# Start-up loads issued from two queues, a high part written in one step, and paced gathers for the second expert in a one-core mixture-of-experts kernel

## The reference, cut to what matters

```python
xprev = concat([shift_state[:, None, :], x[:, :-1]], axis=1)
xk = x + (xprev - x) * time_maa_k
xr = x + (xprev - x) * time_maa_r
e_idx = token_ids * 5099 % 16                 # expert of each of the 8192 tokens
pos = rank of the token within its expert     # kept if pos < 512
expert_in = xk scattered to (16 experts, 512 slots, 512)
h = square(relu(expert_in @ w_key[e]))        # 512 -> 1024
expert_out = h @ w_value[e]                   # 1024 -> 512
r = sigmoid(xr @ w_recept)                    # 8192 x 512 by 512 x 512
out = x + r * expert_out[slot]                # 0 for a token that was dropped
```

## Time and profile before

| | before |
|---|---|
| median of three runs | 886.61 us (886.07 to 887.07) |
| the profiled execution | 886.43 us, of which the span from the first to the last instruction is 884.7 us |
| PE busy | 878.2 us of the span, granted clock 1.0 throughout (the 2.4 GHz level) |
| DVE, ACT, POOL busy | 653.4, 499.4, 502.1 us |
| DMA | 186.40 MB, mean 211 GB/s |

### The profile page before, as it was taken

How to read it: one execution, slowest core, us unless ns; L and a number is a source line. 1 busy time by engine, 2 the same in 40 slices (tenths; PEclk the granted TensorE clock), 3 DMA queues, 4 the chain that set the end, 5 groups by cost and what they waited for, 6 DMA issues and landing times.

```text
span 884.7 us, 10918 instructions
## 1 busy us (share of the span) xinstructions
PE 878.2 (99%) x3963; PEld 726.6 (82%) x3963; DVE 653.4 (74%) x894; ACT 499.4 (56%) x773; POOL 502.1 (57%) x471
## 2 busy tenths in 40 slices
PE   8999999999999999999999999999999999999998
PEld 7888888888888888888888888888888888888887
DVE  6987746859687777777787878787877777777742
ACT  7766656565556464646464737373737282828270
POOL 2000034465676777676767676767676767674142
PEclk9999999999999999999999999999999999999999
DMA  6675568675757575757575757575757565756341
GB/s 240 223 264 194 194 213 281 228 256 164 252 181 252 189 251 186 253 183 251 184 249 180 250 184 244 185 249 185 244 185 243 194 241 190 243 188 223 119 143 47
DMA packets 72533, 186.40 MB, mean 211 GB/s; under 512 B 10400, under 2 KB 10656, under 8 KB 72480
## 3 DMA queue, kind: packets, MB, share of 16 engines
q1 hardware_dynamic: 44672, 101.79, 34.1%
q0 software_dynamic: 27664, 83.91, 28.1%
q10 hardware_dynamic: 144, 0.00, 0.0%
HBM read 152.11 MB, written 33.55 MB: 210 GB/s over the span
## 4 chain that ended last, share of the span: by engine, by line
PE 98%; DMA 0%; issue 0%; DVE 0%; ACT 0%; SPq 0%; POOLq 0%; POOL 0%
PE acc L914 29%; PE acc L916 29%; PE acc L915 29%; PE rt_bank L916 3%; PE rt_bank L914 3%; PE rt_bank L915 3%; PE acc L926 1%; DMA xT<-xs_t 0%; PE rt_bank L994 0%; POOLq L99 0%; POOL out L446 0%; DVE mix L769 0%; ACT mix L502 0%; ACT xr_hi L510 0%; DVE gate L837 0%
## 5 line engine op out<-in xcount | busy, mean ns | idle before, releaser
L431 POOL DMA_INDIRECT pair_even<-pairs,row_pair x128 | 144.6, 1130 | 174.9 <-DVE row_pair L743 105.3
L543 ACT ACTIVATE hid<-acc 128x512 f32<-128x512 f32 x112 | 67.1, 600 | 208.3 <-PE acc L916 208.2
L431 POOL DMA_INDIRECT pair_odd<-pairs,row_pair x128 | 144.9, 1132 | 58.3 <-issue 32.9
L915 PE MATMUL acc<-wv_lo,h_hi 128*128 128x512 f32 (+1 forms) x456 | 176.6, 387 | 0.0
L916 PE MATMUL acc<-wv_hi,h_lo 128*128 128x512 f32 (+1 forms) x456 | 176.6, 387 | 0.0
L914 PE MATMUL acc<-wv_hi,h_hi 128*128 128x512 f32 (+1 forms) x456 | 176.6, 387 | 0.0
L914 PE MATMUL acc<-xk_hi,wk_hi 128*128 128x512 f32 x448 | 174.6, 390 | 0.0
L916 PE MATMUL acc<-xk_hi,wk_lo 128*128 128x512 f32 x448 | 174.5, 390 | 0.0
L915 PE MATMUL acc<-xk_lo,wk_hi 128*128 128x512 f32 x448 | 174.3, 389 | 0.0
L780 DVE TENSOR_TENSOR wv_lo<-raw,wv_hi 128x1024 fp32r<-128x1024 f32 x64 | 78.4, 1226 | 59.5 <-ACT wv_hi L531 59.5
L808 DVE TENSOR_TENSOR h_lo<-hid,h_hi 128x512 fp32r<-128x512 f32 x128 | 88.4, 691 | 35.2 <-ACT h_hi L552 35.2
(11 more groups left out here) (148 smaller groups left out, 1507.3 us busy)
## 6 DMA issues: line engine op xcount, KB each, us to landing
raw<-w_key SPq DMA_DIRECT2D x64, 512.0 KB, 5.5
raw<-w_value SPq DMA_DIRECT2D x64, 512.0 KB, 3.8
xT<-xs_t SPq DMA_DIRECT2D x13, 1026.0 KB, 7.6
gates<-gate SPq DMA_DIRECT2D x8, 1024.0 KB, 5.5
gates<-wr_raw SPq DMA_DIRECT2D x8, 1024.0 KB, 5.3
xT<-xs_t SPq DMA_DIRECT2D x11, 256.5 KB, 5.4
pair_even<-pairs,row_pair POOLq DMA_INDIRECT x128, 3.1
pair_odd<-pairs,row_pair POOLq DMA_INDIRECT x128, 2.9
```

Source lines behind the costliest of these rows:

```text
L431: pool.indirect_dma_start(pair[e % 2][:, i, :], None, pairs, bass.IndirectOffsetOnAxis(row_pair[:, a:a + 1], 0)).then_inc(s_pair[e % 2], 16)
L543: act.activation(hid[:, n % H_SLOTS, :], up_bank(*divmod(n, KF))[:, :], ACT.Relu).then_inc(s_relu, 1)
L915: pe.matmul(bank, hi, m_lo, start=False, stop=False)
```

## The change

It has two parts. At the start, W0 and W1 are issued by ACT, around `maar`, in place of SP, so SP's list is L, R, X1, X2, W2, X3, W3 and so on. DVE writes the high part of the left half directly (the same sum once more, with a rounded output) ahead of writing it to `mix`; POOL, which rounded it, now rounds the right half of W0's chunk, which DVE did. DVE takes `mix_xr(0)` ahead of `split_w_recept(0)`, and PE takes the right half's high by high product ahead of the left half's with `wr_lo`. In the middle, the 16 gathers of the second expert wait, eight per five chunks, for PE's chunks of groups 14 and 15 and its first three blocks of expert 0; PE counts the chunks on a new semaphore `s_chunk`, where `s_R` doesn't.

```diff
             sp.dma_start(xT[:, 0, 0, 0:1 + HALF], xs_t[0:P, 0:1 + HALF]).then_inc(s_x_left, 16)
-            load_w_recept(0)
-            load_group(0, 0)
-            for k in range(1, KD):
+            for k in range(KD):
                 load_group(0, k)
-                load_w_recept(k)
+                if k > 1:
+                    load_w_recept(k)
...
-            pool.wait_ge(s_mix_left, 1)
-            pool.tensor_copy(xr_hi[:, 0, 0, 0:HALF], mix[:, 0, 0:HALF]).then_inc(s_hi_left, 1)
+            pool.wait_ge(s_wrec[0], 16)
+            pool.tensor_copy(wr_hi[:, 0, D // 2:D], wr_raw[:, 0, D // 2:D]).then_inc(s_wrhi_first, 1)
...
+                    elif e == 1:
+                        at = 1 + 5 * i // 8
+                        if at < KD - 1:
+                            pool.wait_ge(s_chunk, at + 1)
+                        elif at == KD - 1:
+                            pool.wait_ge(s_R, ST * (G - 1))
+                        elif at < 2 * KD - 1:
+                            pool.wait_ge(s_chunk, at)
+                        elif at == 2 * KD - 1:
+                            pool.wait_ge(s_R, ST * G)
+                        else:
+                            pool.wait_ge(s_U, at - 2 * KD + 1)
...
+            act.dma_start(wr_raw[:, 0, :], w_recept_t[0:P, :]).then_inc(s_wrec[0], 16)
             act.dma_start(maar[:, :], maa_r[:, :]).then_inc(s_maar, 16)
+            act.dma_start(wr_raw[:, 1, :], w_recept_t[P:2 * P, :]).then_inc(s_wrec[1], 16)
...
                 dve.wait_ge(s_maar, 16)
+                dve.scalar_tensor_tensor(xr_hi[:, 0, 0, 0:HALF], slot, factor, here,
+                                         ALU.mult, ALU.add).then_inc(s_hi_left, 1)
                 dve.scalar_tensor_tensor(slot, slot, factor, here, ALU.mult, ALU.add).then_inc(s_mix_left, 1)
...
             mix_left()
-            dve.wait_ge(s_wrec[0], 16)
-            dve.tensor_copy(wr_hi[:, 0, D // 2:D], wr_raw[:, 0, D // 2:D]).then_inc(s_wrhi_first, 1)
             split_left()
+            mix_xr(0)
             dve.wait_ge(s_wrhi_first, 1)
             split_w_recept(0)
-            mix_xr(0)
...
+                pe.wait_ge(s_hi_right, 1)
+                first_pass(0, right, xr_hi, wr_hi, True)
                 pe.wait_ge(s_wrlo, 1)
                 first_pass(0, left, xr_hi, wr_lo)
-                pe.wait_ge(s_hi_right, 1)
-                first_pass(0, right, xr_hi, wr_hi, True)
                 first_pass(0, right, xr_hi, wr_lo)
...
+                if g + 2 >= G and k < KD - 1:
+                    mm.then_inc(s_chunk, 1)
```

More of the change, by code:

```diff
@@ L280, in moe_token_shift @@
         s_step = sem("s_step")
+        s_chunk = sem("s_chunk")
         s_sq = sem("s_sq")
@@ L760, in split_left @@
                 dve.wait_ge(s_hi_left, 1)
+                dve.wait_ge(s_mix_left, 1)
                 dve.tensor_tensor(xr_lo[:, 0, 0, 0:HALF], mix[:, 0, 0:HALF],
```

## The result

| | before | changed |
|---|---|---|
| median of 11 runs | 886.65 us (886.07 to 887.07) | 888.77 us (887.97 to 889.39) |
| the profiled execution | 886.43 us, span 884.7 | 888.83 us, span 887.1 |
| ratio, 95% interval | | 1.0025 [1.0016, 1.0033] |

What follows compares the result with a forecast made beforehand. PE was taken to bound the kernel, busy 878.2 of 884.7 us. The sum was 886.6 - 0.3 (X1 landing earlier) + 0 (ACT, `maar`, chunk 0) + 0 (gathers) = 886.3 us, range 885.5 to 887.5.

Steps and rivals of the forecast that it cites:

- a block of fixed length: Everything from 8.85 us on: PE busy throughout to 875 us, so only the moment chunk 1 begins moves the end.
- the cover that was named: Second expert's gathers: the last lands by 194.1 to 196.6, at least 2.9 us before DVE wants it; cost nothing.
- ACT's two more issues: Start, on ACT: two added load issues push the table load from 1.24 to 2.2 us, with about 0.35 us cover; cost nothing.
- the two queues fill each other's gaps: Rival at the start: X1 lands by 5.8, chunk 0 then decides, 885.65 to 885.9 us; chance 0.14.
- `maar` behind W0: Start, ACT's queue: `maar`, issued second, lands at 3.9 (bounds 3.3 and 4.2), PE starts at about 4.55; cost nothing.
- the forecast 4.55: PE's first product, on the left half of chunk 0: start at about 4.55 us, where it was 4.59 before.
- the floor of chunk 0: Before chunk 1: PE can't go on before about 8.15 however early X1 lands, limiting the gain to 0.7 us.
- POOL's rounding of the right half: Chunk 0, after `mix_xr(0)`: POOL's rounding takes 0.4 us, its subtraction 0.74, before the right low part is ready.
- W1 goes ahead of X1: Rival at the start: W1 delays X1 by 0.66 or 1.06 us, giving 887.3 or 887.7 us; chance 0.2.
- The slower side: Outcomes later than before: W1 ahead of X1 at the start, chance 0.2; slower by more than 1.8 us, 0.04.
- every rival at the start: X1's landing: no earlier, 886.6 us, chance 0.2; later behind W1, 0.2; by 5.8 with gaps filled, 0.14.
- the signs of being wrong that were named: Whole kernel: PE idles anywhere after the start, or the start moves by more than 1 us either way.

Runs made afterwards that it cites:

- loads alone: Kernel before with only the loads issued as in the change, old steps and no new gather waits: 888.03 us against 886.99.
- gathers alone: Kernel before with only the paced gathers of the second expert and the new count on PE: 886.78 us against 886.99.
- steps alone: Changed kernel with all loads issued as before, so the reordered steps and the paced gathers remain: 887.05 us against 887.08 for the kernel before.
- short warm-up: Kernel before with 14 warm-up matmuls in place of 28, nothing else: 887.36 us against 887.08.
- needed loads in front: Changed kernel with SP issuing L, W0, X1, ACT `maar`, R, W1, only the direct high part kept: 887.55 us; with 38 warm-up matmuls 886.40.
- `maar` first: Changed kernel with `maar` issued first on ACT, then W0 and W1: 887.73 us against 886.99 for the kernel before.

## Why the prediction was wrong

**What held.** The kernel's body after the start is a block of fixed length, and nothing in it moved. The gathers cost nothing, with the cover that was named. ACT's two more issues ended at 2.2 and cost nothing. X1 did land early in the changed kernel, by about 5.8, as in the case called "the two queues fill each other's gaps". The bytes agree with that case: from 2.0 to 6.5 us the engines moved 293 GB/s in the changed kernel and 247 before. But with the loads alone, in the same order, ACT's step on X1 waited until 6.81, so it isn't early in every run.

**The step that failed first: "`maar` behind W0".** Its bounds were 3.3 and 4.2, with 3.9 taken. It landed at 4.87 and was used at 4.96 (4.87 to 5.12 in the five runs with these loads). The upper bound counted L and W0 as all that stands in front, because those two were in by 4.06 before. But `maar` landed 0.2 us after R (about 4.65), which was issued on the other queue at the same moment. It came in as if it stood behind L, W0 and R. The same paragraph gave no price to the wait for L; it came at 4.08 and not at 2.94. A bound that fits is the landing of everything issued by the time `maar` is; that the later loads held it up is inferred from these landings, since no run removes R or X1. So the first product came 1.26 us later than the forecast 4.55. The price in the kernel's time, with the longer warm-ups and the new steps, is 0.65 to 0.75 us.

**The step that was missing: the clock.** The text put the floor of chunk 0 at "8.15 to 8.2", every matmul at 0.23 us, and took the granted clock of 1.00 as given. It read the row of 8.85 to 875 and applied it to 4.6 to 8. Chunk 0 ended at 11.19. With 42 warm-up matmuls and the full level it ended at 9.73, so 1.46 us of the miss are the clock's, and of the other 1.5 us the late first product makes 1.2 and POOL's slow rounding, below, about 0.4. The pause of 1.58 us between warm-up and first product and the idle stretches after it were followed by about 3.4 us at the 1.2 GHz level. The Trainium skill, "TensorE: Matmul & The Clock Gate", section "What's actually happening", says that the throttled state is the default and that activity releases it. The runs agree in so far as the change of the warm-up alone moves the changed kernel by 1.3 to 1.8 us. A forecast that moves the first product later than the last warm-up matmul has to price this. And the clock at the first product differs between runs whose timing there is nearly the same (0.74 us for the first pair at 4.59 before, 1.19 at 4.63 with the gathers alone), so it is a spread as well as a cost.

**A smaller one.** POOL's rounding of the right half was put at 0.4 us; next to a DVE step with two inputs it took 0.80 (changed kernel and steps alone), and 0.40 in the kernel before, when DVE was idle. The reorder put the two side by side. The Trainium skill, "SBUF — State Buffer", section "SBUF: two separate sides", says that DVE and GpSimd share a port pair as an exclusive lock, and that a DVE instruction with two SBUF inputs and a GpSimd one that reads SBUF wait for each other's whole instruction. The trace agrees: POOL's rounding ended 0.26 us after the end of DVE's `wr_lo` both in the changed kernel (7.78 and 7.52) and in the steps alone (6.69 and 6.43). With the old loads the cost is hidden behind X1 (0.1 us); in the changed kernel it stands in the chain, as the 0.81 us piece at 6.98.

**The rivals.** "W1 goes ahead of X1" named the right side and the wrong load: X1 was not late. The slower side got too little, 0.2 and 0.04 for slower by over 0.2%, because every rival at the start looked at X1 alone. Of the signs of being wrong that were named, one came true: the start moved by more than 1 us, by 2.34. The rule that was weighed (the Trainium skill, "DMA: Bandwidth & Descriptors", section "Issuing engines are not separate DMA queues"), that several queues save only issue time, was on the right side of the forecast. But the runs show more than it says: all eight profiled runs on two queues moved 283 to 314 GB/s from 2.0 to 6.5 us, the six on one queue 229 to 256, and yet in each of the eight one of the loads that the first product needs came later than in any of the six.

**And the gain itself.** The -0.3 us rested on one landing of X1, 6.55. With the loads as before, other profiled runs show ACT starting on X1 at 5.73 (short warm-up), 5.86 (before with 34), 6.38 (steps alone), 6.53 (steps with 34) and 6.54 (gathers alone). The quantity that was to be improved by 0.3 varies by 0.8 from run to run, so no such gain could have been read from one trace.

## What to carry to other kernels

At the start of a kernel, look first at when the loads land that the first product needs. Here a second queue moved more bytes in the first microseconds, but they were those of later loads, and the needed ones came later, the 2 KB of `maar` too. When the first product moves, look at the warm-up again: here a warm-up sized for the old start cost 1.3 to 1.8 us. Size it from the trace each time the start is edited, and check the length of the first matmuls, since in two kernels a warm-up that ran without a gap into the first product still left them at the lower level. A longer warm-up also narrowed the spread of the runs, from 1.4 us to 0.24 in the changed kernel and to 0.4 with the needed loads in front, but only to 1.0 in the kernel before.

## What the runs showed of the hardware that was not expected

- A load of 2 KB took 3.63 us from issue to landing as second on its queue (changed kernel), against 2.3 us (before) to 2.9 us (needed loads in front) as first.
- With two issuing queues the engines moved more in 2.0 to 6.5 us (293 GB/s in the changed kernel, 247 before), and the loads issued first landed later all the same (L at 4.08 and not 2.94).
- The granted clock column prints 1.00 for the first microseconds also where the matmuls are at the lower level: in the run with `maar` first a pair took 1.19 us, in the kernel before with 34 warm-up matmuls 1.22, and in the one with the short warm-up 1.06 us, against 0.63 at 7.37 before. In that stretch the length of a known matmul is the better gauge.
- The lower level also came at the first product after a warm-up without a gap (34 matmuls, pairs of 1.22 and 1.20 us), and it came in the middle of chunk 0 after two pairs at the full level (changed kernel, 0.70 at 5.81 and 1.91 for four at 8.63).
- In the kernel before, 34 warm-up matmuls in place of 28 gave 886.53 against 887.01 us, ratio 0.9994 [0.9985, 1.0003]. The interval doesn't settle whether the 0.5 us are real, nor do the profiles say that they would be the clock's: this run had its first two pairs at the lower level, and ACT's step on X1 at 5.86 and not 6.55.
